# Two row tiles of a head pair's attention handled as one 384-column unit, with a new order of the period

## The reference

```python
qkvs = x @ W_qkv.T                       # six projections: qu, ku, vu, qc, kc, vc
term1 = where(causal_mask, 0.0, qc_s @ vu.T)
lookahead = where(causal_mask, sigmoid(qu_s @ ku.T), 0.0)
Su = term1 @ lookahead.T
Sc = qc_s @ kc.T
scores = where(causal_mask, neg, Sc - silu(Su))
attn = softmax(scores, axis=-1)
out = (attn @ vc) @ W_out.T
```

## Time and profile before

| what | value |
|---|---|
| median of three runs | 2072.64 us (2069.22 to 2074.92) |
| the profiled execution | 2075.78 us |
| its span from first to last instruction | 2074.3 us, so 1.5 us lie around it |
| mean granted TensorE clock | 0.976 of full speed |
| PE busy | 1988.0 us, 96% of the span |
| DVE, ACT, POOL busy | 1117.5, 997.2, 699.8 us |
| start until the first period | 152.4 us |
| five periods in a row (batches 1 to 5) | about 182.2 us each |
| period of batch 6 | 194.8 us |
| from the attention of batch 7 to the end | 643 us |

### The profile page before, as it was taken

The page is one execution under the profiler, slowest core; times in us unless marked ns, Lnnn a source line. Parts: engine busy times, 40 slices in busy tenths (PEclk is TensorE's granted clock), DMA queues, the critical chain, the costliest instruction groups (busy, mean ns, idle before and its releaser), DMA issues.

```text
span 2074.3 us, 30776 instructions
## 1 busy us (share of the span) xinstructions
PE 1988.0 (96%) x11224; PEld 1322.1 (64%) x11224; DVE 1117.5 (54%) x2976; ACT 997.2 (48%) x2110; POOL 699.8 (34%) x850
## 2 busy tenths in 40 slices
PE   6769999999999999999999999998999999999998
PEld 4435655655665565566557556644676678888887
DVE  4354574667467566746756574687444437323321
ACT  2325665575666557556655755563454521111111
POOL 2102343334234333423433342333334323333332
PEclk9769999999999999999999999999999999999999
DMA  3020000001000000100000010004112033333333
GB/s 106 0 94 1 1 11 26 22 1 36 1 21 11 27 21 2 36 1 21 9 28 21 2 36 1 21 2 148 48 26 62 11 94 74 78 75 79 74 79 66
DMA packets 59562, 76.68 MB, mean 37 GB/s; under 512 B 7107, under 2 KB 52686, under 8 KB 59158
## 3 DMA queue, kind: packets, MB, share of 16 engines
q1 hardware_dynamic: 46310, 57.15, 8.4%
q0 software_dynamic: 12288, 16.79, 4.8%
q10 hardware_dynamic: 816, 0.79, 0.1%
HBM read 53.58 MB, written 21.00 MB: 36 GB/s over the span
## 4 chain that ended last, share of the span: by engine, by line
PE 91%; DVE 5%; issue 1%; POOL 1%; ACT 1%; DMA 1%; SPq 0%; POOLq 0%; DVEq 0%; ACTq 0%
PE bank L825 13%; PE bank L1039 10%; PE bank L1052 10%; PE bank L889 7%; PE bank L839 4%; PE bank L944 4%; PE bank L913 4%; PE bank L926 4%; PE bank L651 3%; PE bank L901 3%; PE bank L957 3%; PE bank L810 3%; PE bank L677 3%; PE bank L875 2%; PE bank L772 2%; PE bank L719 2%
## 5 line engine op out<-in xcount | busy, mean ns | idle before, releaser
L825 PE MATMUL bank<-hT,wqkv 128*128 128x512 f32 x640 | 302.5, 605 | 1.1 <-ACT hT L1109 1.1
L1831 POOL TENSOR_TENSOR s<-s,ri 128x256 f32<-128x256 f32 (+3 forms) x128 | 162.6, 1271 | 334.7 <-DVE ri L1600 334.6
L1281 ACT ACTIVATE h<-bank 128x512 f32<-128x512 f32 x128 | 76.4, 597 | 345.9 <-PE bank L1039 345.6
L1039 PE MATMUL bank<-xin,ew 128*128 128x256 f32 x1024 | 240.4, 387 | 0.0
L1052 PE MATMUL bank<-ew,h 128*128 128x256 f32 x1024 | 229.4, 382 | 0.0
L1052 PEld LDWEIGHTS bank<-ew,h 128*128 128x128 f32 x1024 | 195.2, 191 | 31.4 <-issue 4.9
L1039 PEld LDWEIGHTS bank<-xin,ew 128*128 128x128 f32 x1024 | 191.8, 193 | 30.2 <-issue 6.4
L1258 ACT ACTIVATE s<-s,mn 128x128 f32<-128x128 f32 (+3 forms) x256 | 141.7, 554 | 142.5 <-DVE mn L1594 142.3
L1869 POOL DMA_INDIRECT out<-y,indices x64 | 102.7, 1604 | 275.6 <-DVE y L1743 189.7
L825 PEld LDWEIGHTS bank<-hT,wqkv 128*128 128x128 f32 x640 | 114.6, 192 | 110.6 <-issue 106.2
L1803 POOL TENSOR_SCALAR look<-look 128x256 f32<-128x256 f32 (+3 forms) x128 | 108.2, 846 | 219.9 <-ACT look L1224 219.2
(11 more groups left out here) (250 smaller groups left out, 3683.8 us busy)
## 6 DMA issues: line engine op xcount, KB each, us to landing
ew<-L_ffn_w SPq DMA_DIRECT2D x24, 1024.0 KB, 8.6
x<-L_attn_x SPq DMA_DIRECT2D x8, 512.0 KB, 4.0
x_scratch<-x SPq DMA_DIRECT2D x8, 512.0 KB, 2.9
x1s<-x_scratch SPq DMA_DIRECT2D x8, 512.0 KB, 5.6
out<-x1s SPq DMA_DIRECT2D x8, 512.0 KB, 2.9
xn_scratch<-n_xn SPq DMA_DIRECT2D x8, 512.0 KB, 2.9
wqkv<-w_qkv SPq DMA_DIRECT2D x1, 3072.0 KB, 10.0
wqkv<-L_wmod SPq DMA_DIRECT2D x2, 1024.0 KB, 8.5
```

Of the source, the lines that this page charges most:

```text
L825: mm = te.matmul(banks[i][:, :], b1.wqkv[:, kk, j * CH1 + hp * P:j * CH1 + (hp + 1) * P], b1.hT[:, kk, :], start=(kk == 0), stop=(kk == KC ...
L1039: mm = te.matmul(banks[i][:, f * 2 * P:(f + 1) * 2 * P], w1[:, kk, (2 * n + f) * P:(2 * n + f + 1) * P], xin[:, kk, :, :].rearrange("p h s ...
L1831: g.tensor_tensor(sc, sc, b1.ri[u % 2][:, :].unsqueeze(2).to_broadcast([P, 2, w]), ALU.mult).then_inc(s["weighted"], 1)
```

## The change

The first two row tiles of a head pair become one unit. `UNIT_TILES = ((0, 1), (2,), (3,))`: unit 0 of a pair holds tile 0 in columns 0 to 127 and tile 1 in columns 128 to 383, units 1 and 2 are tiles 2 and 3 as before. A batch has 12 units, with widths 384, 384 and 512. All three kinds have each head's data in a bank of its own.

For the merged unit the same matmuls are issued, with the same sizes, for both tiles one behind the other. The tanh, the (tanh + 1) * Su, the mask and the copy of the transposes become one instruction per head over 384 columns (the mask one for both heads and both tiles). The row minimum, the exponential and the scaling need a value of their own for each tile and stay one per tile, in a row; mn, sums and ri get room for two tiles. The double buffering now counts these units. `term`, `look`, `proj` and `w` are as before.

`PERIOD` is written anew for the 12 units; the other steps in it are the same but many stand elsewhere. `attention_chunks`, which orders batch 7, puts `w` of half 0 between `su` and `sw` of the merged unit, and has other weights and other places for the projections.

```diff
+UNIT_TILES = ((0, 1), (2,), (3,))
+NV = len(UNIT_TILES)
+NU = NHP * NV
+TILE_AT = (0, P, 0, 0)
+WIDTH = (3 * P, 3 * P, 4 * P)
...
 PERIOD = """
-    -weigh:15 proj:0.0 proj:0.1 proj:0.3 proj:0.4 -attend:14 +x0:0 +stats:0 +norm:0 -turn:15 proj:0.2 -attend:15
+    proj:0.0 proj:0.2 +x0:0 -x1_load:0 -attend:10 -weigh:11 proj:0.3 +stats:0 +norm:0 +ga0_load:0 turn_vu:0 proj:0.1
...
     for n in range(NU):
-        hp, t = n // NT, n % NT
+        hp, u = n // NV, n % NV
         steps = [("weigh", b, n - 1)] if n >= 1 else []
-        yield False, 0.5 + 0.45 * t, steps + [("su", b, n), ("sw", b, n)]
-        yield t < NT - 1 or hp + 1 == NHP, 0.4 + 0.5 * t, [("sc", b, n)]
-        if t == NT - 1 and hp + 1 < NHP:
+        steps.append(("su", b, n))
+        if u == 0:
+            steps.append(("w", b, (hp, 0)))
+        yield False, 0.9 + 0.45 * u, steps + [("sw", b, n)]
+        yield u < NV - 1 or hp + 1 == NHP, 0.9 + 0.5 * u, [("sc", b, n)]
+        if u == NV - 1 and hp + 1 < NHP:
             yield from look_chunks(b, hp + 1)
...
-        if t < 2:
-            yield True, 0.8 + 0.4 * t, [("w", b, (hp, t))]
+        if u == 0:
+            yield True, 1.2, [("w", b, (hp, 1))]
...
         elif step == "su":
...
+            for h in range(2):
+                i, nth = at[step, b, n, h]
+                te.wait_ge(drained[i], nth - 1)
+                for t in tiles:
+                    w = (t + 1) * P
+                    te.matmul(banks[i][:, TILE_AT[t]:TILE_AT[t] + w], b1.term[:, h, t * P:(t + 1) * P],
+                              b1.look[:, h, off(t):off(t) + w], start=True, stop=(t == 0))
...
         elif step == "turn":
...
+                for j in range(WIDTH[n % NV] // P):
+                    mm = te.transpose(banks[i][:, j * P:(j + 1) * P], b1.s[g % 2][:, h, j * P:(j + 1) * P],
+                                      c_.ident[:, :])
+                mm.then_inc(full[i], 1)
...
         elif step == "sc":
...
+                for m, t in enumerate(UNIT_TILES[n % NV]):
+                    sc = b1.s[g % 2][:, h, TILE_AT[t]:TILE_AT[t] + (t + 1) * P]
+                    done = a.activation(sc, sc, ACT.Exp, bias=b1.mn[g % 2][:, m, h:h + 1], scale=-1.0,
+                                        accum_out=b1.sums[g % 2][:, m, h:h + 1])
+                done.then_inc(s["exp"], 1)
...
         elif step == "weigh":
             u = b * NU + n
-            w = (n % NT + 1) * P
             g.wait_ge(s["inverse"], u + 1)
-            sc = b1.s[u % 2][:, :, 0:w]
-            g.tensor_tensor(sc, sc, b1.ri[u % 2][:, :].unsqueeze(2).to_broadcast([P, 2, w]), ALU.mult
-                            ).then_inc(s["weighted"], 1)
+            for m, t in enumerate(UNIT_TILES[n % NV]):
+                w = (t + 1) * P
+                sc = b1.s[u % 2][:, :, TILE_AT[t]:TILE_AT[t] + w]
+                done = g.tensor_tensor(sc, sc, b1.ri[u % 2][:, m, :].unsqueeze(2).to_broadcast([P, 2, w]), ALU.mult)
+            done.then_inc(s["weighted"], 1)
```

230 lines of the change are left out of this document (92 added, 138 removed).

## The result

| | before | after |
|---|---|---|
| median of 8 runs each, taken together | 2071.3 us (2067.2 to 2075.0) | 2079.7 us (2076.6 to 2085.4) |
| ratio after to before | | 1.0044, 95% interval 1.0026 to 1.0062 |
| span of the profiled execution | 2074.3 us | 2076.5 us |
| start until the first period | 152.4 | 145.0 |
| first six periods together | 1084.1 | 1083.0 |

The changed kernel is slower by 0.44%, 8.4 us, clear of the noise by its interval; the forecast was 13 us faster, 2060 us in a range of 2050 to 2066. (The last row ends at PE's last matmul. The 643 us shown for the kernel before run on to the end of the span.) The start differs from one execution to the next: over the 18 profiled executions of this study it lies between 143.4 and 152.4 us, whatever the order behind it, so the 7.4 us of this pair are not the change's.

A forecast was written before the change was run, and what follows sets the result against it. PE was taken to bind, busy 181.5 of 182.3 us a period. Terms -16.3 - 5.6 + 2.1 + 2.8 + 4 = -13.0 us, from 2075.8 to 2062.8 profiled; median forecast 2060 us, range 2050 to 2066.

The forecast's parts named there:

- short covers: Steady periods: little PE work between some products and their readers (look, sc); +0.3 us a period, +2.1 us for seven.
- the choice in batch 6's period: Last stretch of batch 6's period: DVE binds, PE waits 15.2 us for 12.4 before; +2.8 us, between 0 and +8.
- A change of shape: PE's array switching between full, column halves and row halves: 89 fewer switches at 0.19 us; -16.3 us, between -13 and -19.
- The wait from `cn2` to `cn3`: Third cycle of each period: PE's visible wait for the gelu goes; 0.8 us off in seven periods, -5.6 us.
- rival 1: Short covers cost more than counted, 1.3 us a period more, 9 us in all: 2069 us; chance 0.10.
- The merged unit's chain: From a merged unit's sw to its turn: about 7.3 us, covered by at least 10.7 us of PE work; costed at nothing.
- The table loads: ACT: gelu and exp alternate 4 times a period for 8, saving ACT 5.1 us, covered by PE's time; no gain.
- the tighter packing: Batch 6's period: 16 top over 23 us of PE work, 39 before; if it holds up whole chains, +8 us.
- `w` before `sw` in batch 7: Batch 7: a new PE wait of 1.0 us at sw in each of four pairs; +4 us, between +2 and +7.
- 13 changes: Batch 7's attention: 62 switches of the array's shape for 75 before, each priced at 0.19 us.

The follow-up runs named there:

- e6_pool_apart: Changed kernel with weigh:5 ahead of term:2, look:2.3 behind sw:6, proj:3.4 ahead of attend:4; 2088.3 us, ratio 1.0073 to the kernel before.
- e7_w_first: Changed kernel with the first w of each pair ahead of su in batch 7; one execution, 1923.6 us from the first period on, no timed median.

## Why the prediction was wrong, step by step

Two of its terms failed: the short covers of the new order in the steady periods (+0.3 us a period, and some 2.4 more than that came), and the choice in batch 6's period (+2.8 us, measured as 10.1).

- **A change of shape at 0.19 us, 11 fewer a period.** Right: 0.21 by ten that were put in, and 2.1 us less at the changes for the 11 that went. The working behind it was less sound: it gave all the time between columns and waits to the changes, and 8.1 us of it lie at borders of the same shape. That their price came out right all the same is in part luck.
- **The wait from `cn2` to `cn3`.** Right, it is gone. But the parenthesis behind it, "its cycle start has 5.8 us where it had 5.2", took the chain behind `cn4` as unchanged. It grew by 2.0 us through POOL's operations beside it, and made a wait of 1.20 us.
- **Short covers at +0.3 us a period.** This step failed, as rival 1: with the term before it, visible waits were to fall by 0.5 us and rose by 1.0, through two of 1.20 and 0.58, and borders of the same shape grew by another 1.0. Together they took 2.4 of the 2.6 us that the period was to gain. For the first wait the cause is shown: the covers were held against durations of an engine with nothing beside it. The wait of `term` for its bank (0.58 us) stood in none of them, and the 1.0 us at the borders has no shown cause.
- **The merged unit's chain.** Right: no wait at a merged unit's `turn` in the steady periods.
- **The table loads.** Right: ACT's 6.3 us a period less changed nothing.
- **The choice in batch 6's period, +2.8 us.** This step failed by most: +10.1. DVE's work was estimated well (50.7 us, measured 51.3). (16 times 1.42 is a little more than the earlier trace rows give, 0.675 + 0.667 = 1.34; it changes nothing.) The term was 53.1 - 37.9 = 15.2 us of waiting, and 57.7 - 35.2 = 22.5 was measured. Of the 7.3 us between them 2.7 are PE's work: what is left at the first `top` was taken from its place in the order, 37.9 us, while the 49.4 us of before came from the trace, where the first `top` stands later than its place since its rows come by a transfer (DVE idle for 2.0 us before it in the changed kernel); measured in the same way it is 35.2. And 4.0 are DVE's busy share, carried over as 95.5% and measured as 51.3 / 57.7 = 89%. The last 0.6 is DVE's work. On PE's side of the same 22.5 us the clock wasn't counted: 6.3 of it, for 1.7 of 12.4 before. The upper bound of +8 for this term, given for "the tighter packing", came near.
- **`w` before `sw` in batch 7, +4 us.** Right in size: four waits of 0.86 us, and the distance to `feat_t` 1.1 us longer, where the forecast's two terms (4.0 less 13 changes) make 1.5. That the sums agree so well is luck: all of PE's waits in this part are 4.7 us more than before, and the changed kernel's execution happened to be at half the clock for 13.7 us where the kernel before's was for 17.1.
- **Sum.** Six periods: -1.2 us, forecast -15. Batch 6's: +9.7, forecast +0.8. Batch 7: +1.1, forecast 1.5. Rival 1 with its 9 us and the choice's upper bound together would have given 2074; each had been weighed by itself, as if only one of them could come. Both come of an order with less PE work between the same steps.

## What to carry to other kernels

When an order is made shorter, look at what stands in it at fixed counts or fixed places: the work that was spread over the long order gets denser, and a stretch where another engine is full pays for it at once, and the more if PE's waits there bring its clock down. Cost such a stretch from the time of its first instruction in the trace, not from its place in the list. And hold a cover against the chain with its new neighbours: what DVE does with two inputs from SBUF is not the same length beside POOL's work.

## What the runs showed of the hardware

- Some of DVE's instructions take far longer beside POOL's: a tensor_scalar of 512 columns took 0.55 us alone, 1.60 beside a POOL tensor_tensor and 1.27 beside a POOL select (e6_pool_apart), two tensor_tensor on SBUF 1.29 and 2.22 us; copies out of a bank kept their length.
- After 3.44 us without a matmul PE's next ones ran at half the clock (1.02 to 2.01 us for the same two), and in batch 6's stretch half the clock cost 6.3 us of 22.5.
- The clock also fell with no wait over 0.66 us in the 7 us before (e7_w_first, ten matmuls 4.46 us for 2.98), and not in every execution of the same order: in batch 7's part PE was at half the clock for 13.7 to 20.5 us in nine kernels with one order, and the part took 636.5 to 641.3 us.
- A change of the array's shape costs 0.21 us of PE, measured by adding ten; at the 64 to 75 changes of a period the starts lie 0.10 to 0.24 us further apart than the columns take, nearly everywhere.
- The start of this program takes between 143.4 and 152.4 us from one execution to the next, as long as the difference that was to be measured; comparing part by part, from the first period on, is exact to some 0.1 us in the steady periods, and not in batch 7's part.
